# Decoder block on one core: Sinkhorn chains regrouped to 6, 7 and 3 rows, split spectra for every row, five matmuls with no use, last stores on two queues

## The reference, cut to what matters

```python
# x: (16, 128, 1024)
x = x + attention(layernorm(x))                 # 32 heads, 8 kv heads, causal, rotary
# autocorrelation, per row, 8 heads of 128 features, over the 128 tokens
qf, kf = fft(q), fft(ctx)
corr = ifft(qf * conj(kf)).real
w, idx = top_k(corr, 9); w = softmax(w)         # out = sum_i w_i * v[min(idx_i + pos, 127)]
x = x + out
# mixing, per token: logits for a 4x4 matrix, 4 pre and 4 post weights
Z = (x_norm @ W_res.T + H_res_base) / 0.1
for _ in range(50):                             # Sinkhorn
    u = -logsumexp(Z + v, axis=-1); v = -logsumexp(Z + u, axis=-2)
H_res = (1 - g) * I + g * exp(Z + u + v)
x = x + einsum(H_res, streams) + einsum((streams . softmax(pre)) @ W_branch, softmax(post))
```

## Time and profile before

| | before |
|---|---|
| median of 3 runs (lowest to highest) | 1187.41 us (1184.54 to 1189.84) |
| the profiled execution | 1188.75 us |
| its span, first to last instruction | 1186.9 us |
| mean granted clock of TensorE | 0.937 |
| PE busy | 1028.0 us (87%) |
| DVE busy | 907.4 us (76%) |
| ACT busy | 599.3 us (50%) |
| POOL busy | 448.0 us (38%) |

### The profile page before, as it was taken

One profiled execution on the slowest core, in us unless ns is written; L12 is line 12 of the kernel. 1 busy time (PEld: TensorE's weight loads), 2 busy tenths in 40 slices (PEclk: granted clock), 3 DMA queues, 4 the chain that ended last, 5 costly groups with the idle time before them and its releaser, 6 DMA issues. The chain is left out here.

```text
span 1186.9 us, 23294 instructions
## 1 busy us (share of the span) xinstructions
PE 1028.0 (87%) x7874; PEld 762.4 (64%) x7874; DVE 907.4 (76%) x2830; ACT 599.3 (50%) x1787; POOL 448.0 (38%) x665
## 2 busy tenths in 40 slices
PE   5889999999999999999956999999899899833328
PEld 4667777777778777787745677776555565422215
DVE  6756876667866678666563787789999999899993
ACT  6624555435554455544464676775566554421215
POOL 0714433334332344333342675674443343103011
PEclk9989999999999999999968999999999999855759
DMA  9111111110111101110122133233222221119407
GB/s 378 44 43 41 38 60 60 54 48 18 60 60 60 42 18 59 60 60 26 43 109 107 54 101 101 79 98 111 76 94 76 76 92 48 40 36 338 124 4 192
DMA packets 47234, 95.71 MB, mean 81 GB/s; under 512 B 5952, under 2 KB 30400, under 8 KB 47168
## 3 DMA queue, kind: packets, MB, share of 16 engines
q1 hardware_dynamic: 47168, 94.91, 23.6%
HBM read 64.48 MB, written 27.26 MB: 77 GB/s over the span
## 5 line engine op out<-in xcount | busy, mean ns | idle before, releaser
L689 POOL TENSOR_TENSOR prob_G<-prob_G,rl 128x512 f32<-128x512 f32 x96 | 99.7, 1040 | 251.2 <-DVE rl L570 251.2
L436 ACT ACTIVATE prob_G<-prob_G,negm 128x128 f32<-128x128 f32 x384 | 148.8, 389 | 83.4 <-DVE negm L512 83.4
L291 PE MATMUL ps_qkv<-w_hi,xT_hi 128*128 128x512 f32 x384 | 156.4, 407 | 17.4 <-DVE prob_G L575 9.2
L292 PE MATMUL ps_qkv<-w_lo,xT_hi 128*128 128x512 f32 x384 | 151.1, 394 | 0.0
L293 PE MATMUL ps_qkv<-w_hi,xT_lo 128*128 128x512 f32 x384 | 150.9, 393 | 0.0
L365 PE MATMUL ps_qkv<-wo_hi,aT_hi 128*128 128x512 f32 x256 | 109.3, 427 | 0.0
L367 PE MATMUL ps_qkv<-wo_hi,aT_lo 128*128 128x512 f32 x256 | 103.2, 403 | 0.0
L366 PE MATMUL ps_qkv<-wo_lo,aT_hi 128*128 128x512 f32 x256 | 103.2, 403 | 0.0
L291 PEld LDWEIGHTS ps_qkv<-w_hi,xT_hi 128*128 128x128 f32 x384 | 72.7, 189 | 43.2 <-issue 20.2
L508 DVE TENSOR_TENSOR prob_G<-ps_s,mask 128x512 f32<-128x512 f32 x96 | 64.9, 676 | 43.5 <-PE ps_s L274 43.0
L537 DVE TENSOR_TENSOR xT_lo<-ps_t,xT_hi 128x512 fp32r<-128x512 f32 x16 | 11.1, 692 | 101.5 <-ACT xT_hi L475 101.5
(11 more groups left out here) (292 smaller groups left out, 2684.0 us busy)
## 6 DMA issues: line engine op xcount, KB each, us to landing
xin<-in_x SPq DMA_DIRECT2D x16, 512.0 KB, 3.3
xres<-in_x SPq DMA_DIRECT2D x16, 512.0 KB, 4.9
x<-xres SPq DMA_DIRECT2D x16, 512.0 KB, 2.7
c_xin<-x SPq DMA_DIRECT2D x16, 512.0 KB, 4.3
c_b_xres<-x SPq DMA_DIRECT2D x16, 512.0 KB, 3.2
rows_x<-c_row SPq DMA_DIRECT2D x64, 128.0 KB, 2.3
m_xm<-rows_x SPq DMA_DIRECT2D x16, 512.0 KB, 7.7
out<-m_ot SPq DMA_DIRECT2D x64, 128.0 KB, 2.2
```

What stands on the lines that cost most here:

```text
L291: nc.tensor.matmul(ps_qkv[:, n, :], xT_hi[:, k, :], w_hi[:, k, cols], start=k == 0, stop=False)
L292: nc.tensor.matmul(ps_qkv[:, n, :], xT_hi[:, k, :], w_lo[:, k, cols], start=False, stop=False)
L436: r = nc.scalar.activation(prob(g)[:, j, :], prob(g)[:, j, :], ACT.Exp, bias=negm[:, h:h + 1], accum_out=lsum[:, h:h + 1])
L689: nc.gpsimd.tensor_tensor(prob(g), prob(g), rl[:, g * GROUP:(g + 1) * GROUP].rearrange("p (j o) -> p j o", o=1).to_broadcast([P, GROUP, T] ...
```

## The change

Six things change.

1. `ROWS_OF_CHAINS` is (6, 7, 3) for (5, 8, 3): row 5 moves from chain b to chain a.
2. `one_a` begins in body 7 instead of 6, advances 32 steps instead of 40 in a late body (37 in body 12, where the block of logarithms now lies, which was in body 10 with 41 steps), and 32 in body 14. It stands at step 239 of 308 when the ending starts; the other 69 are issued there, in turn with `one_b`, and its last logarithms move behind `shares(n)` on ACT.
3. `whole(n)` is never true: rows 9 to 15 are split as rows 0 to 8 are.
4. Before `select(one_b)` PE issues 3 and then 2 matmuls of 128x512 f32 into a free bank, whose result nothing reads. The first three wait for step 286 of `one_b`, the other two for step 303.
5. The four stores of the last row are issued by two queues: two by SP, two by ACT.
6. `bank_free` for that bank is waited for ahead of these matmuls.

```diff
--- before.py
+++ after.py
@@ -21,7 +21,7 @@
 C = D // NS
 NLOG = NS * NS + 2 * NS
 SINKHORN_ITERS = 50
-ROWS_OF_CHAINS = (5, 8, 3)
+ROWS_OF_CHAINS = (6, 7, 3)
 LOOPED = 4
 TAU = 0.1
 RMS_EPS = 1.1920929e-07
@@ -950,24 +950,23 @@
             for k, part in enumerate((5, 6, 1, 7, 2)):
                 logs_at[b, part] = ((chain, k + 1),)
 
-        begun_in(6, one_a)
-        steps_to[6, 4] = ((one_a, 10),)
+        begun_in(7, one_a)
+        steps_to[7, 4] = ((one_a, 10),)
         at = 10
-        for b in range(7, B - 2):
-            if b == 10:
-                parts = {0: at + 3, 1: at + 9, 2: END[0], 3: END[1], 4: END[1] + 10}
+        for b in range(8, B - 2):
+            if b == 12:
+                parts = {0: at + 2, 1: at + 7, 2: END[0], 3: END[1], 4: END[1] + 14}
                 logs_at[b, 2] = ((one_a, 6), (one_a, 7), (one_a, 8))
             else:
-                parts = {0: at + 3, 1: at + 9, 2: at + 29, 4: at + 40}
+                parts = {0: at + 2, 1: at + 7, 2: at + 23, 4: at + 32}
             for part, to in parts.items():
                 steps_to[b, part] = ((one_a, to),)
             at = parts[4]
         begun_in(B - 2, one_b)
-        steps_to[B - 2, 0] += ((one_a, at + 3),)
-        steps_to[B - 2, 1] += ((one_a, at + 9),)
-        steps_to[B - 2, 2] += ((one_a, END[2]),)
-        steps_to[B - 2, 4] = ((one_b, 14),)
-        logs_at[B - 2, 2] += ((one_a, 9), (one_a, 10))
+        steps_to[B - 2, 0] += ((one_a, at + 2),)
+        steps_to[B - 2, 1] += ((one_a, at + 7),)
+        steps_to[B - 2, 2] += ((one_a, at + 23),)
+        steps_to[B - 2, 4] = ((one_a, at + 32), (one_b, 14))
 
         block = ctx.enter_context(nc.Block())
 
@@ -994,7 +993,7 @@
 
         def whole(n):
 
-            return isinstance(n, int) and n >= 9
+            return isinstance(n, int) and n >= B
 
         def weights_first(b):
 
@@ -1413,7 +1412,6 @@
                 normalised_row(n - 1)
                 branch_copy(n - 2)
                 branch_out(n - 2)
-                log(one_a, FIRST_LOGS + 2 * BLOCK_LOGS, FIRST_LOGS + 2 * BLOCK_LOGS)
                 row_turned(n - 1)
                 act.wait_ge(x2_bias_done, n + 1)
                 nc.scalar.activation(squares[:], x2[:], ACT.Square, bias=x2_bias[:], scale=1.0 / D ** 0.5,
@@ -1425,6 +1423,7 @@
                 branch_copy(n - 1)
                 branch_out(n - 1)
                 shares(n)
+                log(one_a, FIRST_LOGS + BLOCK_LOGS + 1, FIRST_LOGS + 2 * BLOCK_LOGS)
                 branch_copy(n)
                 branch_out(n)
 
@@ -1559,7 +1558,7 @@
                 n = LAST
 
                 def fill(count):
-                    advance(dve, one_b, one_b.issued + count)
+                    weave(dve, (one_b, one_b.issued + count), (one_a, min(END[2], one_a.issued + count)))
 
                 def both(count):
                     weave(dve, (one_b, one_b.issued + count), (one_c, one_c.issued + count))
@@ -1602,7 +1601,6 @@
                         nc.vector.scalar_tensor_tensor(xp[:], row[m % 2][:, i * C:(i + 1) * C], he[:, i:i + 1], xp[:], ALU.mult, ALU.add).then_inc(xp_step, 1)
                         both(1)
 
-                advance(dve, one_a, END[3])
                 fill(2)
                 dve.wait_ge(ws_ps, 2 * n + 1)
                 dve.wait_ge(v_done, 2 * n + 2)
@@ -1627,12 +1625,12 @@
                 fill(14)
                 gate_logits(n)
                 dve.wait_ge(lg_done, n + 1)
-                weave(dve, (one_c, FIRST), (one_b, one_b.issued + FIRST))
+                weave(dve, (one_c, FIRST), (one_b, one_b.issued + FIRST), (one_a, min(END[2], one_a.issued + FIRST)))
                 branch_in(n - 1)
                 gate_max(n)
-                both(12)
+                weave(dve, (one_b, one_b.issued + 12), (one_c, one_c.issued + 12), (one_a, END[2]))
                 branch_in(n)
-                both(22)
+                weave(dve, (one_b, one_b.issued + 22), (one_c, one_c.issued + 22), (one_a, END[3]))
 
             iterations(dve, body, ending)
 
@@ -1798,7 +1796,7 @@
                 else:
                     sp.wait_ge(out_done, NS * LAST + 2 * (n + 1 - LAST))
                     sp.wait_ge(out_by_dve, 2 * (n + 1 - LAST))
-                for i in range(NS):
+                for i in range(NS if n < B - 1 else 2):
                     sp.dma_start(out[n].rearrange("(g t) d -> t g d", g=NS)[:, :, i * C:(i + 1) * C],
                                  ot[n][i * W:(i + 1) * W, :, :]).then_inc(stored[n % 2], 16)
             for i in range(2):
@@ -1862,6 +1860,12 @@
             for n in range(B):
                 if n == one_b.first_row:
                     branch_part(n)
+                    bank_free(NS * (n + 1) - BANKS)
+                    for step, count in ((BASES[2] - 22, 3), (BASES[2] - 5, 2)):
+                        pe.wait_ge(one_b.step, step)
+                        for i in range(count):
+                            nc.tensor.matmul(p_out[NS * (n + 1) % BANKS][:, :], sel_sb[:, 0, :],
+                                             sel_sb[:, :, :].rearrange("p g t -> p (g t)"), start=True, stop=True)
                     select(one_b)
                 elif n == LAST - 2:
                     branch_part(n)
@@ -1909,6 +1913,11 @@
             take_out(LAST - 4, LAST - 2)
             copies(one_c)
             take_out(LAST - 2, B)
+            act.wait_ge(out_done, NS * LAST + 2 * (B - LAST))
+            act.wait_ge(out_by_dve, 2 * (B - LAST))
+            for i in range(2, NS):
+                nc.scalar.dma_start(out[B - 1].rearrange("(g t) d -> t g d", g=NS)[:, :, i * C:(i + 1) * C],
+                                    ot[B - 1][i * W:(i + 1) * W, :, :]).then_inc(stored[(B - 1) % 2], 16)
 
         @block.vector
         def _(dve):
```

## The result

The changed kernel took 1185.6 us in the median of 20 runs (1181.8 to 1190.2), the kernel before 1188.7 beside it (20 runs): a ratio of 0.9973, interval 0.9964 to 0.9982. That is 3.1 us faster, clear of the noise, and a little under half of the forecast's 6.6. Three repeats gave 0.9959 (0.9944 to 0.9975), 0.9971 (0.9956 to 0.9985) and 0.9974 (0.9960 to 0.9989). A few executions, among them the traced one of the version without the useless products (1521.7 us), ran far longer at a lower granted clock and stand in no comparison.

A forecast was written before the change was run, and what follows sets the result against it. PE was taken to bound bodies without chain steps, DVE the late bodies from 7, DVE's chain b mixing, then PE's row products. Terms summed to -6.6 us, from the median 1187.4 to 1180.8 us; range 1172 to 1188.

The forecast's parts named there:

- an ordinary body loses 8 steps, -1.5: Bodies 8 to 13: eight fewer chain steps, priced at 0.19 us each, make an ordinary body 1.5 us shorter.
- Bodies 8 to 13 with no wait on DVE: Expected sign in the late bodies: they take 25.0 us and DVE never waits.
- POOL's pieces at 0.5 us a body: Bodies 8 to 13: eight added POOL pieces delay DVE's chain multiplies, +0.5 us a body.
- The split gains nothing while DVE is the bound: Bodies 8 to 13: the split lowers PE from 24.48 to 22.32 us, which gains nothing.
- The wait at the start of body 14: Body 14: DVE's wait for the key spectrum goes with PE earlier, -1.1 us.
- The two queues: After chain b: issuing the last row's four stores from two queues, -1.0 us.
- The useless products: After chain b: added matmuls raise PE's clock, -2.9 us before chain c's wait, net taken as -0.5.
- ACT's wait for chain c: After chain b: ACT sits in chain c's logarithms, so PE stands 2.1 us between rows 9 and 10.
- Rival 4: Bodies 8 to 13: POOL's pieces cost +1.6 us a body instead of +0.5, whole gain gone, 1187.4 us; chance 0.10.
- Rival 1: Late bodies fall further, wider steps hidden and POOL's pieces meeting no multiply: 6.6 us more, 1174.2; chance 0.25.
- Rival 2: Ending: 69 steps paid in full at 0.19 us, 13.1 instead of 5.2 us, 1188.7 in total; chance 0.12.
- Rival 3: After chain b: ACT's wait for chain c lowers the clock again, +3.8 us, 1184.6 in total; chance 0.08.

The follow-up runs named there:

- 7: Changed kernel, rows 9 to 15 unsplit, three chain a steps moved behind the residual in late bodies except 12, and in 14: 1178.5 us, 0.9906.
- 11: As 7, with one more step ahead of the residual in body 10: 1176.8 us without the split, 1180.0 with it.
- first trace: Traced execution of the unaltered changed kernel, taken with its first measurement: 1183.4 us.
- 4: Kernel before with rows 9 to 15 split, POOL's low parts cut to one column: 1190.6 us; ACT's high parts cut too: 1190.5 us.
- 9: Unaltered changed kernel repeated for a third and fourth trace; the fourth traced execution took 1185.5 us.
- 5: First split matmul issued twice in bodies 8 to 14: kernel before with the split 1194.0 us, changed kernel 1185.6 us.
- fourth trace: Traced execution from the last repeat of the unaltered changed kernel, at the median: 1185.5 us.
- 2: Changed kernel with rows 9 to 15 unsplit (f32) again: 1181.5 us, 0.9932 of the kernel before.
- 8: Changed kernel with its split, three steps moved behind the residual: 1178.9 us; with rows 9 to 15 unsplit and five moved: 1179.0 us.
- 10: Changed kernel, rows 9 to 15 unsplit, without useless matmuls and second store queue: 1181.7 us; changed kernel without useless matmuls only: 1186.4 us.

## Why the prediction was half right

**The step that failed: "an ordinary body loses 8 steps, -1.5".** The price of 0.19 us was the mean over the 40 steps of a body. It isn't the price of these eight: three of them stood behind the residual, where ACT's work sets the length and a step is free (7). Without the split bodies 8 to 13 gained 1.4 us where the forecast's terms without POOL's pieces give 5.9. Three steps moved back brought 2.5 of the 4.5 missing in the bodies. Another 1.0 or so is where the cut falls: body 7 came out at 21.96 us instead of 22.9 and body 8 longer by 0.8 than body 9, the two together at 47.8 as forecast, since PE is 0.8 us further behind DVE at the cut between them than at the next. About 1 us of the 4.5 has no cause here. The stall taken out of body 10 (11) was worth 1.1 more, but the forecast had counted on that stall, so it is a gain of its own. The earlier trace rows held the hint: in body 4 DVE waits 2.5 us for `c_k_spec` and in body 9 not at all; I took that wait for covered and did not ask how much of the cover I was removing. "Bodies 8 to 13 with no wait on DVE" was wrong for the same reason.

**The second: what the split costs.** I priced POOL's pieces at 0.5 us a body, and they took 0.4 (the chain multiplies take 2.4 us more over bodies 8 to 13 in the first trace than without the split) to 0.56 (4). That term was right. "The split gains nothing while DVE is the bound" was wrong in sign: the 1.5 us that PE saves in a body (24.2 against 22.7 in body 9) it spends standing. With DVE late beside POOL's pieces the clock falls more often, and PE's next products hold up ACT and DVE (9). That both are needed fits 4 and 5; the pieces beside f32 products were not tried. Fourth trace against the version without the split: +3.3 in bodies 8 to 13, +0.6 in body 14, +1.3 in mixing up to chain b's end, -0.1 in the ending, -0.7 behind it, 4.3 in all with the 0.1 of bodies 5 to 7; the stretch up to body 5, which the split does not touch, was 1.2 shorter in that trace. By the ratios the split costs 3 to 5 us here (2), and 2.5 with the steps moved (7 and 8), 3.2 by the medians of 11. The wait at the start of body 14, which I had the split remove, went without it too (0.16 us left in the first trace, 0.17 without the split). Of the 1.3 in mixing 1.0 lies ahead of chain a's coefficients; it stays without POOL's and ACT's part of the split, and its cause was not sought.

**Two small terms.** The two queues brought 0.2 us in the mean of the traces instead of 1.0. The useless products ended PE's work 0.4 us earlier in the one pair of traces that differs by the two edits, and up to 1.5 in others, where 0.5 was forecast (10). Where the clock stayed high, ACT's wait for chain c took part of it back, as the forecast had it (1.67 us of standing, forecast 2.1). The times show neither term.

**What held.** In mixing, from chain a's second `m_coef` to chain b's, it is 69.4 us instead of 73.1. Behind it one row less was left. The stall moved to body 10 alone, as counted (1.53 us there). Other terms were mis-sized to the good: the ending cost 3.1 to 3.9 instead of 5.2, body 14 0.9 to 1.8 instead of 2.1, and bodies 6 and 7 gained 3.8 instead of 2.9. In the fourth trace these offset 2.6 of the 4.8 us missing in bodies 8 to 13, so that the miss in the bodies was larger than the total shows.

**The rivals.** Rival 4 named the right place, but its price was for multiplies that wait, and these cost what was forecast; what else went with the pieces was as large. Rival 1 did not come true in any version: the ordinary bodies 9 to 11 never fell below 24.2 us. Rival 2 was the other way round, the ending being cheaper than forecast. Rival 3's fall of the clock was there in the late bodies; at the end PE stood 1.67 us in two of the four traces and the clock stayed high.

## What to carry to other kernels

The mean price of an instruction is not the price of the ones you remove: before counting a saving, look at where they stand, and measure the distance between the two events around them that another engine fixes; if it doesn't change with their number, they are free there, and belong there. Shortening an engine that isn't the bound can cost time, when it then stands more, and the clock falls just ahead of work that others wait for. Try the parts of a bundle apart: here the regrouping was worth nearly 8 us, the split cost 3 to 5 of them, and two edits brought less than the times can show.

## What was new about the hardware

The same gaps of PE, to a hundredth of a microsecond (1.51 and 1.38 us in one execution, 1.52 and 1.37 in another), were followed by products at 2.4 GHz in the one and by 7 us at 1.2 GHz in the other. So the low-clock stretches stand in different places from run to run, three of them in bodies 8 to 13 in each of the four traces, and these bodies take 158.8 to 158.9 or 159.8 us, with 1.0 us or more added behind them where they take longer. PE's short products without POOL's pieces (0.73 us each) brought few of them (two in bodies 7 to 13), both together six. And a chain multiply stalls beside POOL's 1.90 us instruction exactly where it is the step between the two residuals: that happened 24 times in the 19 traces compared here, each time for 1.48 to 1.53 us, and no chain step took over 1 us in any other place of bodies 7 to 13. So it depends on the count of steps: one step more ahead of the residual in one body was worth 1.05 us.
